# Single-head context attention of one sublayer: pairs of batches in plain f32, column halves of the array, keys read turned from DRAM

## The reference

```python
x = x + _L2_xattn_ref(_layernorm(x), ctx_512, ctx_512, Wq, bq, Wk, bk, Wv, bv)
    q = jnp.einsum('bld,de->ble', query, Wq) + bq
    k = jnp.einsum('bld,de->ble', key, Wk) + bk
    v = jnp.einsum('bld,de->ble', value, Wv) + bv
    scores = jnp.einsum('bqe,bke->bqk', q, k)
    attn = jax.nn.softmax(scores, axis=-1)
    out = jnp.einsum('bqk,bke->bqe', attn, v)
```

## Time and profile before

| | us |
|---|---|
| median of 3 runs (lowest, highest) | 5167.7 (5158.91, 5170.9) |
| the profiled execution's own time | 5178.64 |
| its span in the profile | 5176.6 |
| its mean granted TensorE clock | 0.898 |

### The profile page before, as it was taken

The page is one execution under the profiler, slowest core; times in us unless marked ns, Lnnn a source line. Parts: engine busy times, 40 slices in busy tenths (PEclk is TensorE's granted clock), DMA queues, the critical chain, the costliest instruction groups (busy, mean ns, idle before and its releaser), DMA issues. The chain is left out here.

```text
span 5176.6 us, 107578 instructions
## 1 busy us (share of the span) xinstructions
PE 4381.3 (85%) x43346; PEld 3327.0 (64%) x43346; DVE 2742.8 (53%) x5458; ACT 1877.6 (36%) x3952; POOL 797.1 (15%) x485
## 2 busy tenths in 40 slices
PE   6869999999774969999776598776799899997877
PEld 3649888888554946666522497662599666664565
DVE  5447777777253045555459422555333466664543
ACT  1225555555121424444334121430244344443111
POOL 0013222221001010000049301425122000001100
PEclk8789999999866989999888799898799999999885
DMA  1110000000114821111012386329211000000211
GB/s 58 37 31 16 16 24 16 16 16 1 41 41 147 310 67 53 41 41 34 29 46 77 132 316 224 83 60 126 53 48 41 27 28 22 28 16 35 70 38 33
DMA packets 233648, 328.65 MB, mean 63 GB/s; under 512 B 57507, under 2 KB 190964, under 8 KB 215316
## 3 DMA queue, kind: packets, MB, share of 16 engines
q1 hardware_dynamic: 223508, 307.86, 19.7%
q0 software_dynamic: 3072, 8.39, 0.5%
q10 hardware_dynamic: 6624, 6.03, 0.3%
HBM read 265.20 MB, written 31.60 MB: 57 GB/s over the span
## 5 line engine op out<-in xcount | busy, mean ns | idle before, releaser
L2686 DVE TENSOR_REDUCE block_max<-PS 128x1 f32<-128x512 f32 (+1 forms) x896 | 505.7, 628 | 300.7 <-PE PS L2546 300.0
L2635 ACT ACTIVATE probs_turned<-PS 128x512 f32<-128x512 f32 (+1 forms) x896 | 435.5, 572 | 563.6 <-PE PS L2567 563.5
L844 PE MATMUL PS<-context_turned,queries 128*128 128x512 f32 x1728 | 411.7, 382 | 25.5 <-issue 18.7
L876 PE MATMUL PS<-probs_turned,context_part 128*128 128x256 f32 (+2 forms) x3120 | 407.7, 285 | 3.7 <-DVE weighted L953 3.7
L905 ACT CAST probs_turned<-PS 128x512 fp32r<-128x512 f32 x576 | 262.2, 511 | 358.9 <-PE PS L856 358.9
L876 PEld LDWEIGHTS PS<-probs_turned,context_part 128*128 128x128 f32 (+1 forms) x3120 | 381.4, 190 | 4.4 <-DVE probs_turned L919 4.3
L844 PEld LDWEIGHTS PS<-context_turned,queries 128*128 128x128 f32 x1728 | 310.5, 196 | 86.2 <-issue 22.1
L919 DVE TENSOR_TENSOR probs_turned<-PS,probs_turned 128x512 fp32r<-128x512 f32 x576 | 311.1, 582 | 96.9 <-ACT probs_turned L905 94.7
L911 ACT ACTIVATE probs<-PS,minus_max 128x1024 f32<-128x1024 f32 (+1 forms) x288 | 268.8, 936 | 86.4 <-DVE minus_max L964 85.2
L959 DVE TENSOR_REDUCE row_max<-PS 128x1 f32<-128x1024 f32 (+1 forms) x288 | 272.7, 982 | 41.7 <-PE PS L844 41.2
L2587 PEld LDWEIGHTS PS<-probs_turned,values 128*17 128x17 f32 x13312 | 191.4, 97 | 147.7 <-issue 120.8
(11 more groups left out here) (485 smaller groups left out, 7717.5 us busy)
## 6 DMA issues: line engine op xcount, KB each, us to landing
context_rows<-in_ctx SPq DMA_DIRECT2D x40, 768.0 KB
routed_up<-in_L_ffn_W SPq DMA_DIRECT2D x23, 1024.0 KB, 7.4
routed_down<-in_L_ffn_W SPq DMA_DIRECT2D x23, 1024.0 KB, 5.3
routed_up<-in_L_ffn_wg_w SPq DMA_DIRECT2D x23, 1024.0 KB, 7.3
routed_second<-in_L_ffn_w_w SPq DMA_DIRECT2D x23, 1024.0 KB, 9.7
routed_down<-in_L_ffn_w_w SPq DMA_DIRECT2D x23, 1024.0 KB, 4.9
v_all<-v_turned SPq DMA_DIRECT2D x128, 128.0 KB, 19.5
ctx_turned<-context_turned SPq DMA_DIRECT2D x16, 800.5 KB, 4.7
```

The source lines that it names most:

```text
L844: last = nc.tensor.matmul(S[:, 512 * j:512 * j + cols], qs[a][:, v, p * P:(p + 1) * P], yT[b][:, v, 512 * j:512 * j + cols], start=(m == 0 ...
L876: last = nc.tensor.matmul(O_ps, yp[a][0:kk, u, k, :], probsT[b][0:kk, par, k, :], start=(k == 0 and m == 0), stop=(k == KT - 1 and m == 2))
L2635: nc.scalar.activation(probs[0:kk, t % ring, i, 0:many].rearrange("p k c s -> p (k c s)"), PS[0:kk, bank_of("turned", t, i), 0:many * 2 * ...
L2686: nc.vector.tensor_reduce(part[:, b % 2, chunks[0]:chunks[-1] + 1, i, u // 2], bank, AX_X, ALU.max).then_inc(max_done.sem, 1)
```

## The change

`context_rows` makes the two loads of a batch's rows; it gives each partition 12 neighbouring keys instead of every 128th, so a partition's piece is 6144 bytes long. `TurnedContext` uses it too, so the turned context in DRAM has its keys in that order, in which L3_xattn reads it.

`l2_xattn` no longer calls `context_attention`. `PairedContext` holds four slots, each with the turned context and the rows of two batches, 24 loads in all in the block of `normalize`. WkT is applied to all queries in a second `linear_turned`. `pair_attention` takes a tile (two batches) per step, in plain f32: the scores of batch a go to partitions 64a to 64a + 63 of banks 0 to 3, so each product has 64 stationary columns; maxima, exponentials and transposes work on both batches at once; the weighted sums again have two products per key tile, one for each half of the partitions. The result is scaled, turned and multiplied by Wv in token rows, and DVE adds it to x; bv is added to x once, by POOL. The deferred work of the steps is: transposes and sums of step t - 1, scaling, turning and Wv of step t - 2.

```diff
@@ -2332,6 +2332,13 @@
     constants_made.passed(2 * DC + 2 if biased else 1)
+def context_rows(core, b, to, landed):
+    context = core.dram["ctx_512"]
+    return [(to[:, 0:KT - 1, :], context[b, 0:(KT - 1) * P, :].rearrange("(p k) c -> p k c", k=KT - 1), landed),
+            (to[0:KLAST, KT - 1, :], context[b, (KT - 1) * P:KEYS, :], landed)]
 class TurnedContext:
@@ -2348,9 +2355,7 @@
         landed = self.landed[b % 2]
         if not self.first:
             return [(self.y[b % 2][:], core.dram["ctx_turned"][b], landed)]
-        context, t = core.dram["ctx_512"], self.rows[b % 2]
-        return [(t[:, 0:KT - 1, :], context[b, 0:(KT - 1) * P, :].rearrange("(k p) c -> p k c", p=P), landed),
-                (t[0:KLAST, KT - 1, :], context[b, (KT - 1) * P:KEYS, :], landed)]
+        return context_rows(core, b, self.rows[b % 2], landed)
 def head_attention(core, room, Q, made, wv, biased, wo, wo_rows, oT, scale):
@@ -2754,35 +2759,238 @@
             s.passed(16 * BATCH // 2)
+class PairedContext:
+    def __init__(self, core, own, slots):
+        self.slots = slots
+        self.rows = core.sb(own, "context_rows", [P, slots, 2, KT, CDIM])
+        self.turned = core.sb(own, "context_turned", [CDIM, slots, 2, KEYS])
+        self.landed = core.semaphores("pair_landed", slots)
+        self.per_pair = 16 * 2 * 3
+        self.loads = [load for i in range(slots) for load in self.loads_of(core, i)]
+    def loads_of(self, core, i):
+        u, found = i % self.slots, []
+        for a in range(2):
+            found.append((self.turned[:, u, a, :], core.dram["ctx_turned"][2 * i + a], self.landed[u]))
+            found += context_rows(core, 2 * i + a, self.rows[:, u, a], self.landed[u])
+        return found
+def pair_attention(core, room, qT, wv, bv):
+    nc, PS, X = core.nc, core.PS, core.X
+    slots = room.slots
+    turn_bank, o_bank, r_bank = 4, 6, 7
+    halves = (slice(0, 1024), slice(1024, KEYS))
+    fill_tiles = [range(4 * n, min(4 * n + 4, KT)) for n in range(4)]
+    keys_in = lambda k: KLAST if k == KT - 1 else P
+    S = PS[:, 0:4, :].rearrange("p b n -> p (b n)")
...
+        with nc.Block() as block:
+            @block.sync
+            def _(sp):
+                for i in range(slots, TILES):
+                    sp.wait_ge(o_ready.sem, o_ready.at(i - slots + 1))
+                    for dst, src, there in room.loads_of(core, i):
+                        sp.dma_start(dst, src).then_inc(there.sem, 16)
...
+            @block.tensor
+            def _(pe):
+                def scores(i):
+                    u = i % slots
+                    pe.wait_ge(room.landed[u].sem, room.landed[u].at(room.per_pair * (i // slots + 1)))
+                    for half in range(2):
+                        if i:
+                            pe.wait_ge(e_done.sem, e_done.at(2 * i - 1 + half))
+                        for j in (2 * half, 2 * half + 1):
+                            cols = min(512, KEYS - 512 * j)
+                            for a in range(2):
+                                last = nc.tensor.matmul(PS[a * SEQ:(a + 1) * SEQ, j, 0:cols], qT[:, 0, (2 * i + a) * SEQ:(2 * i + a + 1) * SEQ],
+                                                        room.turned[:, u, a, 512 * j:512 * j + cols], start=True, stop=True)
+                        last.then_inc(s_ready.sem, 1)
+                def turn_exps(i, n):
+                    if n == 0:
+                        pe.wait_ge(e_done.sem, e_done.at(2 * i + 2))
+                    if n == 2:
+                        pe.wait_ge(t_act.sem, t_act.at(i + 1))
+                    elif n == 3:
+                        pe.wait_ge(t_dve.sem, t_dve.at(3 * i + 1))
+                    elif i:
+                        pe.wait_ge(t_dve.sem, t_dve.at(3 * i - 1 + n))
+                    for k in fill_tiles[n]:
+                        kk = keys_in(k)
+                        last = nc.tensor.transpose(PS[0:kk, turn_bank + n % 2, (k - 4 * n) * P:(k - 4 * n + 1) * P],
+                                                   probs[:, i % 2, k * P:k * P + kk], core.ident[:])
+                    last.then_inc(turned.sem, 1)
+                def weighted(i, n):
+                    u = i % slots
+                    if n == 0:
+                        pe.wait_ge(t_act.sem, t_act.at(i + 1))
+                        if i >= 2:
+                            pe.wait_ge(o_taken.sem, o_taken.at(i - 1))
+                    else:
+                        pe.wait_ge(t_dve.sem, t_dve.at(3 * i + n))
+                    for k in fill_tiles[n]:
+                        kk = keys_in(k)
+                        for a in range(2):
+                            last = nc.tensor.matmul(PS[a * SEQ:(a + 1) * SEQ, o_bank, i % 2 * CDIM:(i % 2 + 1) * CDIM],
+                                                    probsT[0:kk, i % 2, k, a * SEQ:(a + 1) * SEQ], room.rows[0:kk, u, a, k, :],
+                                                    start=(k == 0), stop=(k == KT - 1))
+                    if n == 3:
+                        last.then_inc(o_ready.sem, 1)
+                def turn_weighted(i):
+                    pe.wait_ge(o_taken.sem, o_taken.at(i + 1))
+                    if i:
+                        pe.wait_ge(ot_taken.sem, ot_taken.at(i))
+                    nc.tensor.transpose(PS[:, r_bank, 0:P], O[:, i % 2, :], core.ident[:]).then_inc(ot_ready.sem, 1)
+                def project(i):
+                    pe.wait_ge(ot_taken.sem, ot_taken.at(i + 1))
+                    if i:
+                        pe.wait_ge(r_taken.sem, r_taken.at(i))
+                    nc.tensor.matmul(PS[:, r_bank, DIM:2 * DIM], OT[:, i % 2, :], wv[:], start=True, stop=True).then_inc(r_ready.sem, 1)
...
+                for t in range(TILES + 2):
+                    now, before = t - 1, t - 2
+                    if t < TILES:
+                        scores(t)
+                    if 0 <= now < TILES:
+                        turn_exps(now, 0)
+                        turn_exps(now, 1)
+                    if before >= 0:
+                        turn_weighted(before)
+                    if 0 <= now < TILES:
+                        weighted(now, 0)
+                        turn_exps(now, 2)
+                        weighted(now, 1)
+                    if before >= 0:
+                        project(before)
+                    if 0 <= now < TILES:
+                        turn_exps(now, 3)
+                        weighted(now, 2)
+                        weighted(now, 3)
+            @block.scalar
+            def _(act):
+                def exps(i):
+                    act.wait_ge(m_ready.sem, m_ready.at(i + 1))
+                    if i >= 2:
+                        act.wait_ge(turned.sem, turned.at(4 * (i - 1)))
+                    for half, cols in enumerate(halves):
+                        nc.scalar.activation(probs[:, i % 2, cols], S[:, cols], ACT.Exp, bias=bias[:, i % 2:i % 2 + 1],
+                                             accum_out=total[:, i, half:half + 1]).then_inc(e_done.sem, 1)
...
+                for t in range(TILES + 2):
+                    now, before = t - 1, t - 2
+                    if 0 <= now < TILES:
+                        act.wait_ge(turned.sem, turned.at(4 * now + 1))
+                        nc.scalar.copy(probsT[:, now % 2, 0:4, :].rearrange("p k s -> p (k s)"), PS[:, turn_bank, :]).then_inc(t_act.sem, 1)
+                    if before >= 0:
+                        act.wait_ge(ot_ready.sem, ot_ready.at(before + 1))
+                        nc.scalar.copy(OT[:, before % 2, :], PS[:, r_bank, 0:P]).then_inc(ot_taken.sem, 1)
+                    if t < TILES:
+                        exps(t)
+            @block.vector
+            def _(dve):
+                def maxima(i):
+                    for half, cols in enumerate(halves):
+                        dve.wait_ge(s_ready.sem, s_ready.at(2 * i + half + 1))
+                        nc.vector.tensor_reduce(top[:, i % 2, half:half + 1], S[:, cols], AX_X, ALU.max).then_inc(step.sem, 1)
+                    dve.wait_ge(step.sem, step.at(2 * i + 2))
+                    nc.vector.tensor_scalar(bias[:, i % 2:i % 2 + 1], top[:, i % 2, 0:1], top[:, i % 2, 1:2], -1.0, ALU.max,
+                                            ALU.mult).then_inc(m_ready.sem, 1)
+                def normal(i):
+                    dve.wait_ge(e_done.sem, e_done.at(2 * i + 2))
+                    nc.vector.tensor_tensor(inverse[:, i:i + 1], total[:, i, 0:1], total[:, i, 1:2], ALU.add).then_inc(sum_done.sem, 1)
+                    dve.wait_ge(sum_done.sem, sum_done.at(i + 1))
...
+                    dve.wait_ge(o_ready.sem, o_ready.at(i + 1))
+                    nc.vector.tensor_scalar(O[:, i % 2, :], PS[:, o_bank, i % 2 * CDIM:(i % 2 + 1) * CDIM], inverse[:, i:i + 1], None,
+                                            ALU.mult).then_inc(o_taken.sem, 1)
+                for t in range(TILES + 2):
+                    now, before = t - 1, t - 2
```

(35 more changed lines are left out.)

34 lines of the change are left out of this document (added).

## The result

The changed kernel takes 5036.97 us (median of 4 runs, 5025.88 to 5040.82) against 5169.3 us: a ratio of 0.9741, 95% interval 0.9721 to 0.9761. Its profiled execution took 5025.88 us, with a span of 5024.1 us. In the table a sublayer goes from its first weight load to the next one's.

What follows compares the result with a forecast made beforehand. TensorE was taken to set the attention's pace, busy 175.7 of 195.9 us. Savings of 128.2 us in L2_xattn and 2.5 in L1_xattn took 5178.6 to 5047.9; the runs' median, 10.9 lower, gave 5037.0 us, range 5028 to 5062.

Steps and rivals of the forecast that it cites:

- The halves overlap: Pair attention: products of two batches in separate column halves run at once, giving 8.3 us a pair against 22.3.
- Rival (a): Pair attention: the halves don't overlap, a pair takes 13.1 us, 38.0 us more, total 5075; chance 0.14.
- Rival (b): Pair attention: weight loads wait for products, nothing overlaps, a pair takes 17.0 us, total 5106; chance 0.03.
- 0.16 us per block: Pair attention on PE: cost above ideal per block where tiling changes; four blocks in column groups add 0.64 us.
- First pair 5.6 us: Start of pair attention: scores, maxima, minus_max, first exponential and handing over take 5.6 us before the steady turns.
- Block end 14.3 us after the start: L2_xattn's norm block: SP's 24 load issues move its end from 3250.8 to near 3255.0, losing 4.2 us.
- 24 x 0.45 = 10.8 us: SP in L2_xattn's norm block: 24 context load issues at 0.45 us each, since their pieces are long.
- rival (d): L2_xattn's norm block: SP's issues are held up to 3278, 23 us later, total 5060; chance 0.06.
- Projections 15.3 us with their block change: Between norm block and scores: query projection 10.3 us, new projection by WkT 4.7, and 0.3 more.
- rival (c): Pair loop: loads bind at 322 GB/s, 10.2 us a pair, some 4 us late, total 5041; chance 0.07.
- L1_xattn 2.5 us: L1_xattn's norm block: long-piece row loads issue faster, gaining 2.5 us, bounds 0 and 3.3; nothing more in its batches.
- Rival (e): Pair attention: no overlap and PE stays at 1.2 GHz, a pair takes 26.2 us, total 5180, slower; chance 0.01.

Runs made afterwards that it cites:

- the second median: The changed kernel measured once more, unedited, beside its variants: 5048.58 us, ratio 0.9781 to the kernel before.
- Regrouping: Changed kernel with PE's order in a turn regrouped, four changes between whole array and column halves instead of six: 5043.16 us.

## Why the prediction was right, and where its steps were not

Forecast 5037.0 us, measured 5036.97 us. That agreement is closer than the steps earned: the stage saved 114.0 us in the profile, not 128.2, and L1_xattn 8.4, not 2.5, together 122.4 against 130.7. (The spans of these two profiles are 152.5 us apart; the other 30 us lie in sublayers that the change doesn't touch.) The first measurement of the same two kernels had 132 us between its medians, the second 108, so scatter filled the gap, and that the medians agree to 0.1 us is luck; the second median, 5048.58, lies in the range too. The stage's 14.2 us are 10.6 at the norm's block, -0.7 in the projections and 4.3 from the first scores on.

- **The halves overlap:** right, and the decisive step. The 0.007 us between starts show it, and the 5.54 us for scores that all use one half. Rival (a) (no overlap) would have had a turn of 13.1 us.
- **Rival (b), weight loads wait for products:** it did not come. The two halves share all rows, and yet a weight load and an instruction for each half come every 0.109 us; the 0.115 us of the earlier trace rows was the right row to believe. The Trainium skill ("TensorE: Matmul & The Clock Gate", Part 3, The mechanism) says that a weight load overlaps products only in another row group; this trace disagrees.
- **0.16 us per block:** right by size, too few by count. Regrouping measured 0.17 us per change. I counted four blocks, 0.64 us; the turn enters the halves three times and leaves them three times, six changes. With six at 0.16 the sum is 8.3 + 0.32 = 8.6 us, and 8.65 came. (Its 0.2 us of wait for ACT's copy is there in part: in the turn at 3284.62 the copy ends at 3285.90 and the sums start at 3285.95, 0.4 us after the instruction before them.) Seven turns: 2.5 us of the miss.
- **First pair 5.6 us:** right, 5.5. But the next pair's scores, behind a wait of 2.6 us for the exponentials, took 4.54 us instead of 2.87, at a granted clock of 0.63 from 3263.34 to 3267.81 (4.3 to 4.6 us in the other profiles, but for the one with both batches in one half): 1.7 us. With the turns this makes 76.0 us from the first scores to the next sublayer instead of 71.7.
- **Block end 14.3 us after the start:** wrong, and the largest miss: 24.9. The step that failed is "24 x 0.45 = 10.8 us": an issue's price was taken as one of its own pieces, whatever is outstanding. The first 13 context loads took 7.4 us instead of 5.9, the last 11, at the pace of the transfers, 14.7 instead of 5.0. This is rival (d), which I priced at +23 us with the end of the transfers; the hold ends earlier, when the last 1,135 pieces are still under way, so it cost 10.6 us. The two kernels with fewer early loads show it, 16.8 and 10.2 us.
- **Projections 15.3 us with their block change:** 14.6.
- **Loads, rival (c):** right that they cost nothing in the loop. With two slots they cost 10.8 us per turn. The trace shows 397 GB/s over the 19 us from 3224.0 to the block's end. The Trainium skill ("DMA: Bandwidth & Descriptors", Bandwidth) gives 358 GB/s for a core when both cores of a pair load, and 425 for a 16 MB load by one alone; the trace lies between them, and the prediction named only the first.
- **L1_xattn 2.5 us:** its block gave 2.9; "Its batches never waited for rows, so nothing more" was wrong: PE's waits for rows were none, but the steps from batch to batch take some 7 us less with long pieces (568.0 to 570.9 us in ten profiles against 577.1 and 577.7), half of it in idle times whose cause stays open and half in the lower clock behind them.
- **Rival (e), slower at the lower clock:** the steady turns had 1.00. From the first projection on, the lower level came only there and at the second scores, both behind a wait.

## What to carry to other kernels

Products whose stationary side has 64 columns run two at a time when they use different column halves and stand next to each other in PE's order; count a change between whole array and halves, both ways, at 0.17 us. Before loads are moved to the head of a stage, count the pieces that will be outstanding: in these traces, past some 1,100 pieces of 6 KB the issuing engine went at the pace of the transfers, and everything that waits for the end of its block is late; issue what the first steps need, and the rest one block later. A kernel that agrees with its forecast can still hide two misses of opposite sign: read each step.

## What was not expected of the hardware

- The issue of a load is held with 1,133 pieces outstanding (5.8 MB, long pieces), and with short ones until some 1,700 are left (1.5 MB); 1,092 long ones (5.4 MB) did not hold.
- PE starts an instruction for one half up to three instructions ahead of its place in the stream, even the next block's first score beside the last sums.
- Row loads in 512-byte pieces come with longer idle times of PE in L1_xattn, 9.8 us against 5.6 to 6.6, though no product waits for a row.
- One and the same projection took from 8.2 us (granted clock 1.00) to 11.0 us to the next one's start, in one code with equally short waits 8.2 and 10.2: the clock alone moves a stage by 2 to 3 us between profiles.
